# A one-column GpSimd clear before each of the 3,126 row gathers of two edge aggregations

## The reference, cut to what matters

```python
x = x + _L0_gnn_ref(_layernorm(x), src, dst, edge_weight, W, b)
#   msgs = features[edge_src] * edge_weight[:, None]
#   agg  = segment_sum(msgs, edge_dst);  agg @ W.T + b
x = x + _L0_ffn_ref(...)     # eight experts with a capacity, one per token
x = x + _L1_gnn_ref(_layernorm(x), edge_index, edge_weight, ...)
#   row, col = src, dst      # here the sum is by source, the rows come from dst
#   h = x @ W;  agg = segment_sum(edge_weight[:, None] * h[col], row);  batch norm, relu
x = x + _L1_ffn_ref(...)     # a graph attention picks two of four experts per token
```

## Time and profile before

| what | us |
|---|---|
| median of 3 runs | 8039.75 (8026.65 to 8046.51) |
| the profiled execution, its own time | 8028.86 |
| its span | 8027.1 |
| first aggregation: first to last gather start | 195.2 to 2236.2 |
| second aggregation: first to last gather start | 3851.2 to 5885.2 |
| GpSimd busy over the span | 5416.4 (67%) |
| PE / DVE / ACT busy over the span | 5638.6 / 4514.7 / 3750.7 |
| mean granted clock of TensorE | 0.821 |

### The profile page before, as it was taken

The page is one execution under the profiler, slowest core; times in us unless marked ns, Lnnn a source line. Parts: engine busy times, 40 slices in busy tenths (PEclk is TensorE's granted clock), DMA queues, the critical chain, the costliest instruction groups (busy, mean ns, idle before and its releaser), DMA issues. The chain is left out here.

```text
span 8027.1 us, 80843 instructions
## 1 busy us (share of the span) xinstructions
PE 5638.6 (70%) x19687; PEld 3938.3 (49%) x19687; DVE 4514.7 (56%) x8806; ACT 3750.7 (47%) x9645; POOL 5416.4 (67%) x5982
## 2 busy tenths in 40 slices
PE   6555556655667999968466656656658888888857
PEld 5444444444455666644344444444434555555545
DVE  6455555555577999947555555555565222222227
ACT  5666666666662222226465566666544222222214
POOL 4777777777743222236677777777755888888875
PEclk8777777777758999989687787787778999999978
DMA  7333333333331111136333333333325222222228
GB/s 243 101 99 101 101 101 101 103 102 101 102 117 64 53 42 58 42 89 208 101 101 101 101 102 102 101 101 102 101 91 156 57 57 57 57 57 57 58 54 330
DMA packets 498615, 796.88 MB, mean 99 GB/s; under 512 B 121278, under 2 KB 363563, under 8 KB 498059
## 3 DMA queue, kind: packets, MB, share of 16 engines
q0 software_dynamic: 200256, 453.47, 20.8%
q1 hardware_dynamic: 297904, 338.22, 12.9%
HBM read 595.60 MB, written 197.30 MB: 99 GB/s over the span
## 5 line engine op out<-in xcount | busy, mean ns | idle before, releaser
L1008 PE MATMUL part<-rows,spread 128*128 x6656 | 2359.0, 522 | 1658.3 <-ACT spread L1040 1159.5
L1008 PEld LDWEIGHTS part<-rows,spread 128*128 128x128 f32 x6656 | 1702.0, 265 | 2245.7 <-issue 1909.7
L966 DVE TENSOR_TENSOR agg<-agg,part 128x257 f32 (+1 forms) x3328 | 1404.2, 422 | 1765.7 <-PE part L1008 1195.4
L949 POOL DMA_INDIRECT rows<-h,row x1563 | 1557.8, 997 | 506.8 <-issue 475.5
L949 POOL DMA_INDIRECT rows<-f,row x1563 | 1566.1, 1002 | 485.6 <-issue 475.8
L1040 ACT ACTIVATE spread<-spread,weight 128x128 f32<-128x128 f32 x3328 | 1017.3, 388 | 1350.2 <-SPq L932 1303.5
L1949 POOL DMA_INDIRECT rows<-gat,src x1122 | 1077.9, 961 | 185.0 <-issue 185.0
L1032 ACT ACTIVATE spread<-iota,place 128x128 f32<-128x128 f32 x3328 | 1012.4, 387 | 264.6 <-PE part L1008 205.9
L2027 PE MATMUL y_ps<-agg,hid 128*128 128x256 f32 x3136 | 765.7, 405 | 191.9 <-DVE y_all L2157 191.9
L2027 PEld LDWEIGHTS y_ps<-agg,hid 128*128 128x128 f32 x3136 | 641.1, 206 | 343.6 <-DVE y_all L2157 210.8
L405 POOL COPY spare<-pay 128x1024 f32<-128x1024 f32 x105 | 222.3, 2117 | 734.8 <-DVE pay L392 505.9
(11 more groups left out here) (400 smaller groups left out, 6447.3 us busy)
## 6 DMA issues: line engine op xcount, KB each, us to landing
expert_rows<-y_all SPq DMA_DIRECT2D x196, 256.0 KB
made<-expert_rows SPq DMA_DIRECT2D x49, 1024.0 KB, 13.5
x<-x SPq DMA_DIRECT2D x42, 896.0 KB, 7.0
rows<-f,row POOLq DMA_INDIRECT x1563, 2.7
rows<-h,row POOLq DMA_INDIRECT x1563
rows<-gat,src POOLq DMA_INDIRECT x1122
xbuf<-zero SPq DMA_DIRECT2D x16, 1024.0 KB
x<-xbuf SPq DMA_DIRECT2D x32, 512.0 KB, 4.4
```

The lines of the kernel that those rows point to most:

```text
L949: pool.indirect_dma_start(out=rows[:, u, 0:D], out_offset=None, in_=table, in_offset=bass.IndirectOffsetOnAxis(ap=q.row[:, i:i + 1], axis= ...
L966: nc.vector.tensor_tensor(sum_t, sum_t, part[:, p % NB, 0:WIDE], ALU.add).then_inc(added, 1)
L1008: nc.tensor.matmul(part[:, p % NB, 0:WIDE], spread[:, p % (2 * BANKS), :], row_p, start=True, stop=True).then_inc(multiplied, 1)
```

## The change

In `aggregate_edges` GpSimd now writes 0.0 to column 0 of `k.zero` (128 partitions, one float32 each) before each gather. The clear increments a new semaphore, `rested`, and from the second gather on the clear waits until the clear before it has completed. Values stay what they were.

```diff
-        worded = s.sem("worded")
+        worded, rested = s.sem("worded"), s.sem("rested")
...
                     if i >= SPAN and u % BANKS == 0:
                         pool.wait_ge(freed, (i - SPAN) // BANKS + 1)
+                    if i:
+                        pool.wait_ge(rested, i)
+                    nc.gpsimd.memset(k.zero[:, 0:1], 0.0).then_inc(rested, 1)
                     pool.indirect_dma_start(out=rows[:, u, 0:D], out_offset=None, in_=table,
```

## The result

The changed kernel takes 8068.27 us (median of 7 runs, 8058.68 to 8079.94) against 8046.51 us for the kernel before (7 runs, 8026.65 to 8053.31). The ratio is 1.0034 with a 95% interval of 1.0023 to 1.0044: slower by 0.3%, about 27 us. The prediction was 7993 us, 0.6% faster. The profiled execution took 8058.68 us, its span 8056.9 us, 29.8 us over the span before.

What follows compares the result with a forecast made beforehand. The prediction took GpSimd's gather stream to bound both aggregations; 3,126 gathers x 0.79 x 0.019 us gave a gain of 47 us, and 8039.75 - 47 = 7993 us, range 7944 to 8090.

Steps and rivals of the forecast that it cites:

- What bounds the kernel: Both aggregations: GpSimd's gather stream sets their length, and a change of it passes to the end one to one.
- What one gather costs with the clear: Aggregation gather streams: start-to-start distance falls from 1.250 to 1.231 us, a gain of 0.019 us a gather.
- the straight line: Gather distance against clear width, from 256 and 1,792 columns: 0.00083 us per column, 1.231 us at one column.
- the gap is not the clear's to shorten: Between aggregation gathers: the 0.304 us gap overlaps the clear, distance stays 1.250 us, time 8040 us; chance 0.24.
- The wait on the clear before is free: Before each aggregation clear: the earlier clear has completed behind a 0.946 us gather, so the wait costs nothing.
- The slower rival: Between aggregation gathers: the gap stays and the clear's 0.033 us slot is added, 81 us, 8121 us; chance 0.23.
- Waits moved for nothing: Aggregations: moving the wait for free slots from gather to clear costs nothing, since it was met but for 1.6 us.
- The share that DVE holds: Gathers held under two-input DVE operations, 22% and 20% of the streams, gain nothing; the factor on the gain is 0.79.
- The reading of the sorting step: Aggregation sorting step: one gather ends 0.81 us behind L385's end; the next, 0.96 us, fits between L386 and L387.
- Clears held in sorting steps: Sorting steps: a clear only writes, so DVE does not hold it; clears of about a microsecond would show otherwise.

Runs made afterwards that it cites:

- e2_w128: The changed kernel with each clear 128 columns wide instead of one; 8327.32 us in one run.
- e12_lag2_timed: The changed kernel with clears alternating over two columns, each waiting for the clear before the last; 8023.95 us, ratio 0.9995 to the kernel before.
- e13_after: The changed kernel itself, timed again on the same chip as e12_lag2_timed; 8055.53 us, ratio 1.0034 to the kernel before.
- e1_nowait: The changed kernel with clears rotating over 256 columns and waiting for an earlier clear only at every 128th gather; ratio 1.0002 to the kernel before.
- e4_inc: The changed kernel with clears and their waits replaced by a semaphore increment before each gather; 8028.79 us in one run, kernel before 8030.45.

## Why the prediction was wrong

**What bounds the kernel** was right. The length of the gather stream goes through to the end: e2_w128's streams grew by 166 and 136 us against the trace of the kernel before, and its time by 297 us over that kernel on the same chip.

**"What one gather costs with the clear"** was the first step that failed. It took the straight line from 256 and 1,792 columns down to one, 1.231 us, and made a gain of 0.019 us a gather and 47 us of it. The line is right as far as it was later measured, down to 32 columns, but a floor of 1.250 us lies across it. The gain was 0. The rival "the gap is not the clear's to shorten" described this, with its reason: the line's negative fixed cost, odd for added work, was overlap. What was held against it, the same 0.17 behind a clear of 1.60 us, is compatible with it: the larger of two times gives 0.17 behind any clear that is long enough. The forecast should have given more weight to a fixed cost below zero, which is a sign that the fit runs past the end of an overlap.

**"The wait on the clear before is free"** was the second, and it decided the sign. The prediction put it at nothing because the clear that is waited for has completed by then. It has, by the time the engine comes to the next clear; but the sequencer asks earlier. The wait ties it to within about one gather of the engine, and a stop that the kernel before hides then shows for 0.92 us at every 96th gather: 30 us. The runs show the cost and that the wait's reach decides it: the pair e12_lag2_timed and e13_after puts 31.6 us on it, and the 3.61 us from the met wait to the gather give its size. That it works through the run-ahead is a reading, and what the stop itself is stays open. No row of the kernel before could have given the price: its attention loop has the same chain of waits and no stop. No term, bound or rival of the prediction held a cost of this kind, so that the result lay inside the range (8068 of 7944 to 8090) was luck.

**The slower rival** had the sign and not the mechanism: the gather starts did not move from 1.250 us, so nothing was paid for the clear's slot.

**Waits moved for nothing** held: the wait for free slots, now on the clear, came to 2.1 us once. **The share that DVE holds**, 0.79, was a factor on a gain that did not exist; the streams of e1_nowait and e12_lag2_timed, which have no stops, agree with the kernel before within 6 us. For added time e2_w128 puts the factor at 1, so it was wrong as well. The reading of the sorting step behind it was off in one place: the second gather of the earlier trace rows does not fit in a seam, it ends at 1112.45, again 0.82 us behind the end of a DVE operation (L386, at 1111.63). **Clears held in sorting steps** did not occur: of 3,126 clears the longest took 0.291 us, against gathers of up to 2.921 us. That a GpSimd operation which only writes is not held by a DVE operation with two SBUF inputs is what the Trainium skill, SBUF — State Buffer, Who interferes with whom, says, and the trace agrees. By the Trainium skill, GPSIMD Engine Reference, Instruction dispatch, each instruction pays for its dispatch. Here one and two clears ahead of a gather added nothing to its distance of 1.250 us, since they lay inside the 0.304 us.

## What to carry to other kernels

A semaphore wait that is met long before the engine gets to its instruction can still cost time. By the reading above it caps how far a sequencer runs ahead, and whatever the run-ahead was hiding appears; where nothing is hidden, as in the attention loop, it costs nothing. If an order is needed between small instructions of a tight stream, wait on the one two back, with a buffer more: here that took the loss away, since 3.94 us are more than 3.61. And when a straight line through measured sizes gives a negative fixed cost, look for a floor before using the line at the small end.

## What the runs showed of the hardware

- Between two indirect gathers of 128 rows on GpSimd there are 0.304 us in which one or two short clears fit for nothing. The distance of 1.250 us is the same for rows of 1,024 and of 512 bytes. What GpSimd does in the 0.304 us was not shown.
- Every 96th gather, at the same place in both streams, there is a stop: with one clear to a gather, the gather there starts no sooner than 3.61 us behind the end of the clear that stands two gathers ahead. It shows for 0.92 us when a clear waits for the last clear and not at all when it waits for the one before it. It did not move with the number of instructions between gathers (one, two and four clears) or with the bytes of a row, and once it showed for 1.41 us in a kernel without any clear or chained wait (e4_inc, 1,553rd gather). The attention stage's 1,122 gathers, with the same chain of waits, have none. What it is stays open; no gather line in the profile names a cause ("issue").
- In the kernel before, a gather held under a DVE operation with two SBUF inputs ends about 0.82 us behind that operation's end (L385, L386, L856; 0.62 behind the predicated copies L391 and L392). In the changed kernel gathers took up to 2.92 us, and no clear over 0.29.
